# Retention decays: from a mask product per pair to running sums made once and read back as rows

## The reference

```python
q = _l2norm((x @ Wq).reshape(b, seq_len, h, d)).transpose(0, 2, 1, 3)
k = _l2norm((x @ Wk).reshape(b, seq_len, h, d)).transpose(0, 2, 1, 3)
v = (x @ Wv).reshape(b, seq_len, h, d).transpose(0, 2, 1, 3)
dt = jax.nn.softplus(x @ Wa + dt_bias)
alpha = jnp.exp(-jnp.exp(A_log) * dt)
cum_log = jnp.cumsum(jnp.log(alpha + 1e-08), axis=1).transpose(0, 2, 1)
log_l = cum_log[..., :, None] - cum_log[..., None, :]
l_mat = jnp.where(causal, jnp.exp(log_l), 0.0)
scores = jnp.einsum('bhid,bhjd->bhij', q, k) * l_mat
out = jnp.einsum('bhij,bhjd->bhid', scores, v)
...
return out * gate @ Wo
```

## Time and profile before

| | us |
|---|---|
| median of 3 runs (1632.02 to 1636.08) | 1634.42 |
| the profiled execution | 1648.23 |
| its span in the profile | 1646.4 |
| busy in the span: PE 94%, DVE 68%, ACT 54%, POOL 43% | |
| granted TensorE clock, mean over the span | 0.979 |

### The profile page before, as it was taken

The page is one execution under the profiler, slowest core; times in us unless marked ns, Lnnn a source line. Parts: engine busy times, 40 slices in busy tenths (PEclk is TensorE's granted clock), DMA queues, the critical chain, the costliest instruction groups (busy, mean ns, idle before and its releaser), DMA issues. The chain is left out here.

```text
span 1646.4 us, 45308 instructions
## 1 busy us (share of the span) xinstructions
PE 1544.4 (94%) x16414; PEld 1193.2 (72%) x16414; DVE 1121.6 (68%) x1761; ACT 896.3 (54%) x1419; POOL 701.8 (43%) x755
## 2 busy tenths in 40 slices
PE   8998999989999987889999999999999999889998
PEld 4544666679989655457777777777777777668887
DVE  3643545668787468467777777777777777267777
ACT  5463333432222347346666666666666666467776
POOL 0300000577877456443444433444433444166665
PEclk9998999999999999799999999999999999999999
DMA  2028984131110000376655566655556654212211
GB/s 76 1 58 223 249 243 129 39 118 51 64 41 22 1 2 2 90 166 151 145 127 131 129 142 149 147 125 131 129 140 149 149 125 112 52 39 79 69 63 45
DMA packets 53548, 168.84 MB, mean 103 GB/s; under 512 B 12640, under 2 KB 25280, under 8 KB 53472
## 3 DMA queue, kind: packets, MB, share of 16 engines
q1 hardware_dynamic: 51312, 156.30, 38.0%
q10 hardware_dynamic: 2160, 11.52, 2.3%
HBM read 90.27 MB, written 1.03 MB: 55 GB/s over the span
## 5 line engine op out<-in xcount | busy, mean ns | idle before, releaser
L1907 DVE TENSOR_REDUCE hat_tops<-banks 128x1 f32<-128x500 f32 x672 | 442.0, 677 | 151.4 <-PE banks L1653 151.3
L1780 ACT ACTIVATE hat_pb<-banks 125x896 f32<-125x896 f32 x384 | 340.2, 916 | 226.3 <-PE banks L1672 222.2
L1653 PE MATMUL banks<-hat_kh,hat_qm 128*128 128x500 f32 x672 | 298.7, 462 | 3.8 <-DVE hat_tops L1907 3.5
L1672 PEld LDWEIGHTS banks<-hat_q,hat_k 128*125 128x125 f32 x1536 | 219.6, 188 | 74.4 <-issue 31.9
L1672 PE MATMUL banks<-hat_q,hat_k 128*125 128x224 f32 x1536 | 250.5, 286 | 15.8 <-ACT hat_pb L1780 9.2
L1849 POOL CAST hat_kh<-hat_kf 128x500 fp32r<-128x500 f32 x96 | 58.5, 609 | 404.1 <-ACT hat_kf L1793 389.3
L1663 PE MATMUL banks<-hat_pb,hat_vs 125*27 125x168 f32 (+1 forms) x6144 | 166.9, 261 | 0.1
L1663 PEld LDWEIGHTS banks<-hat_pb,hat_vs 125*27 125x27 f32 (+1 forms) x6144 | 132.1, 98 | 44.1 <-issue 24.4
L1226 ACT ACTIVATE ffn_rg<-banks 128x448 f32<-128x448 f32 x128 | 69.9, 546 | 165.6 <-PE banks L1159 165.5
L1653 PEld LDWEIGHTS banks<-hat_kh,hat_qm 128*128 128x128 f32 x672 | 127.7, 191 | 40.9 <-DVE hat_tops L1907 25.5
L2149 DVE TENSOR_TENSOR moe_hl<-moe_hf,moe_hh 128x448 fp32r<-128x448 f32 x128 | 108.5, 887 | 42.3 <-POOL moe_hh L2041 41.6
(11 more groups left out here) (286 smaller groups left out, 3091.3 us busy)
## 6 DMA issues: line engine op xcount, KB each, us to landing
hat_k<-hat_kh SPq DMA_DIRECT2D x256, 187.5 KB, 4.7
hat_ct<-ctxT SPq DMA_DIRECT2D x32, 750.0 KB, 6.2
hat_k<-hat_kl SPq DMA_DIRECT2D x128, 187.5 KB, 4.5
ctx_cx<-ctx SPq DMA_DIRECT2D x32, 672.0 KB
ctx_cd<-ctxT ACTq DMA_DIRECT2D x15, 750.0 KB, 5.7
ffn_cb<-expert_weights SPq DMA_DIRECT2D x8, 896.0 KB, 4.3
moe_cb<-expert_weights SPq DMA_DIRECT2D x8, 896.0 KB, 6.1
moe_raw<-Mw SPq DMA_DIRECT2D x18, 256.0 KB, 3.0
```

Source lines behind the costliest of these rows:

```text
L1653: peak_out.inc(nc.tensor.matmul(g.bank(PK + m % 2)[:, 0:SB], qm[u][:].rearrange("p h i -> p (h i)")[:, r * 128:r * 128 + 128], kh[u][:, c ...
L1672: mm = nc.tensor.matmul(g.bank(2 * (t % 2) + j // 2)[0:SW, (j % 2) * QW:(j % 2 + 1) * QW], k3[u][:, j, t * SW:(t + 1) * SW], q3[u][:, j, : ...
L1780: exped.inc(nc.scalar.activation(pb[t % 6][:].rearrange("p (n i) -> p n i", n=2), g.ps[0:SW, 2 * (t % 2):2 * (t % 2) + 2, 0:2 * QW], ACT.E ...
L1907: peaked.inc(v.tensor_reduce(tops[:, r, n:n + 1], g.bank(PK + m % 2)[:, 0:SB], AX_X, ALU.max))
```

## The change

The running sums of the log decays are made once for all pairs, and each pair's mask product takes them in.

- First block: one product of the selector `until` with all decays (256 columns, fp32) into bank 4, between the first and the second half of the v projections. ACT rounds its negative into `parts`, DVE puts the rounding's remainder beside it, PE turns `parts` in four transposes into bank 5, ACT copies that into `turned` (128 x 4 x 128). SP stores `turned` in DRAM (`sums_dram`), waits for the store, and then issues the four loads of the rows of pairs 0 and 1, all before the block ends.
- POOL fills two tables `hid` (the hiding values for 16 heads; rows 56 to 59 are overwritten by the loads) and `head_of`, and `unit` is no longer the identity: its rows 56 to 59 subtract the loaded rows.
- Second block: SP issues two loads per pair (2 x 16 x 56 numbers each) for pairs 2 to 15, each pair's after PE has finished the masks of the pair two before. PE's first two products read `hid` instead of `hidden` and also wait for the loads; the two fp32 products with `after` and `dm` are replaced by two fp32r products of 32 rows with `turned` and `head_of`. DVE's `dm` is gone, and with it the wait on it.
- The loop `staged` is replaced by `each_pair`, which writes all 18 slots out.

```diff
-    out["after"] = (same & (p[:, None] > p[None])) * 1.0
+    out["until"] = (same & (p[:, None] <= p[None])) * 1.0
+    out["head_in_pair"] = (p[:, None] % H == np.arange(H)[None]) * 1.0
+    rows = np.diag((p % 64 < L) * 1.0)
+    rows[L:L + 2, 0:L] = rows[L + 2:L + 4, 64:64 + L] = -1.0
+    rows[L + 4, L:64] = rows[L + 4, 64 + L:128] = 1.0
+    out["row_of"] = rows
...
+        def load_rows(sp, p):
+            for k in range(2):
+                source = g.sums_dram[p // 4, 32 * (p % 4):32 * (p % 4) + 32, 64 * k:64 * k + L]
+                sp.dma_start(hid[p % 2][L + 2 * k:L + 2 * k + 2].bitcast(F32), source.rearrange("(l h) i -> l h i", l=2)).then_inc(rows_in[p % 2], 16)
...
+                sp.wait_ge(sums_kept, 1)
+                sp.dma_start(g.sums_dram.rearrange("g r c -> r g c"), turned[:].bitcast(F32)).then_inc(sums_stored, 16)
+                sp.wait_ge(sums_stored, 16)
+                sp.wait_ge(cleared, 6)
+                for p in range(2):
+                    load_rows(sp, p)
...
                     if p == 8:
+                        pe.wait_ge(scaled, 3)
+                        pe.wait_ge(s_step, 6)
+                        nc.tensor.matmul(g.bank(4)[:, 0:PAIRS * H], c_["until"], decay[:].rearrange("p a h -> p (a h)"), start=True, stop=True).then_inc(sums_out, 1)
                         pe.wait_ge(limited, CH)
...
+                pe.wait_ge(sums_split, 2)
+                for n in range(4):
+                    mm = nc.tensor.transpose(g.bank(5)[:, n * 128:n * 128 + 128], parts[:, 4 * n:4 * n + 4].rearrange("p a l h -> p (a l h)").bitcast(F32), c_["ident"])
+                mm.then_inc(sums_turned, 1)
...
+                act.wait_ge(sums_out, 1)
+                nc.scalar.activation(parts[:, :, 0, :], g.bank(4)[:, 0:PAIRS * H].rearrange("p (a h) -> p a h", h=H), ACT.Copy, scale=-1.0).then_inc(sums_split, 1)
+                act.wait_ge(sums_turned, 1)
+                nc.scalar.copy(turned[:].rearrange("p g c -> p (g c)"), g.bank(5)).then_inc(sums_kept, 1)
...
+            @block.sync
+            def _(sp):
+                for p in range(2, PAIRS):
+                    d_out.wait(sp, p - 2)
+                    load_rows(sp, p)
...
                         exped.wait(pe, p - 1)
+                        pe.wait_ge(rows_in[u], 32 * (h + 1))
                         for k in range(2):
-                            nc.tensor.matmul(g.ps[:, 4 + k, 0:CW], unit[:], hidden[:], start=True, stop=False)
-                        dmade.wait(pe, p)
+                            nc.tensor.matmul(g.ps[:, 4 + k, 0:CW], unit[:], hid[u][:, 8 * k:8 * k + 8, :], start=True, stop=False)
+                        own_rows = slice(32 * (p % 4), 32 * (p % 4) + 32)
                         for k in range(2):
-                            mm = nc.tensor.matmul(g.ps[:, 4 + k, 0:CW], c_["after"], dm[u][:, 8 * k:8 * k + 8, :], start=False, stop=True)
+                            mm = nc.tensor.matmul(g.ps[:, 4 + k, 0:CW], turned[own_rows, p // 4, :], head_of[own_rows, 8 * k:8 * k + 8, :], start=False, stop=True)
                         d_out.inc(mm)
...
-                    if scores:
-                        d_out.wait(dve, p - 2)
-                        a = decay[:].rearrange("p a h -> p (a h)")[:, bass.ds(p * H, H)]
-                        dmade.inc(nc.vector.tensor_tensor(dm[u][:], spread(a, 2, L), spread(c_["upto"], 1, H), ALU.mult))
...
-                staged(dve, PAIRS, slot)
+                each_pair(dve, slot)
```

More of the change, by code:

```diff
@@ L379, in retention @@
         vm = [sb(f"vm{u}", [128, HG * (D + DH)]) for u in range(2)]
-        unit, hidden = sb("unit", [128, 128], F32R), sb("hidden", [128, CW], F32R)
+        unit, head_of = sb("unit", [128, 128], F32R), sb("head_of", [128, H, L], F32R)
+        hid = [sb(f"hid{u}", [128, H, L], F32R) for u in range(2)]
+        parts, turned = sb("parts", [128, PAIRS, 2, H], F32R), sb("turned", [128, 4, 128], F32R)
+        sums_out, sums_split, sums_turned, sums_kept, sums_stored = (sem(n) for n in ("sums_out", "sums_split", "sums_turned", "sums_kept", "sums_stored"))
+        rows_in = [sem(f"rows_in{u}") for u in range(2)]
+        def load_rows(sp, p):
+            for k in range(2):
+                source = g.sums_dram[p // 4, 32 * (p % 4):32 * (p % 4) + 32, 64 * k:64 * k + L]
+                sp.dma_start(hid[p % 2][L + 2 * k:L + 2 * k + 2].bitcast(F32), source.rearrange("(l h) i -> l h i", l=2)).then_inc(rows_in[p % 2], 16)
         with nc.Block() as block:
@@ L429, in _ @@
                     nc.gpsimd.memset(vm[u][:], 0.0).then_inc(cleared, 1)
-                nc.gpsimd.tensor_copy(unit[:], c_["ident"]).then_inc(cleared, 1)
-                nc.gpsimd.tensor_copy(hidden[:].rearrange("p (h i) -> p h i", i=L), spread(c_["hide_later"], 1, CW // L)).then_inc(cleared, 1)
-                pool.wait_ge(cleared, 4)
+                nc.gpsimd.tensor_copy(unit[:], c_["row_of"]).then_inc(cleared, 1)
+                for u in range(2):
+                    nc.gpsimd.tensor_copy(hid[u][:], spread(c_["hide_later"], 1, H)).then_inc(cleared, 1)
+                nc.gpsimd.tensor_copy(head_of[:], spread(c_["head_in_pair"], 2, L)).then_inc(cleared, 1)
+                pool.wait_ge(cleared, 6)
             @block.scalar
@@ L487, in _ @@
                 dve.wait_ge(scaled, CH)
+                dve.wait_ge(sums_split, 1)
+                nc.vector.scalar_tensor_tensor(out=parts[:, :, 1, :], in0=g.bank(4)[:, 0:PAIRS * H].rearrange("p (a h) -> p a h", h=H), scalar=-1.0,
+                                               in1=parts[:, :, 0, :].bitcast(F32), op0=ALU.mult, op1=ALU.subtract).then_inc(sums_split, 1)
+                dve.wait_ge(sums_split, 2)
         kp = [sb(f"kp{u}", [128, 2 * L]) for u in range(2)]
         qb = [sb(f"qb{u}", [128, 2, HG, L]) for u in range(2)]
-        dm = [sb(f"dm{u}", [128, H, L]) for u in range(2)]
         ee = [sb(f"ee{u}", [128, H, L]) for u in range(2)]
@@ L548, in slot @@
                         scored.inc(mm)
-                staged(pe, PAIRS, slot)
+                each_pair(pe, slot)
             @block.scalar
@@ L1931, in _, with each_pair @@
                 normed.wait(dve, B - 1)
+def each_pair(engine, slot):
+    for p in range(PAIRS + 2):
+        slot(p, p % 2, p // 2, p < PAIRS, 1 <= p <= PAIRS, p >= 2)
 def staged(engine, n, slot):
```

12 lines of the change are left out of this document (6 added, 6 removed).

## The result

The changed kernel takes **1657.97 us** in the median of 4 runs (1653.54 to 1669.1), beside 1634.62 us in 4 runs of the kernel before on the same chip: a ratio of **1.0141, 95% interval 1.0106 to 1.0176**. It is slower by 23.4 us, 17.3 to 28.8, where 7.0 us less were forecast. Its profiled execution takes 1658.55 us, near its median. In the experiments each ratio is taken against the kernel before run beside it (medians 1636.71 to 1640.01 us). One slow execution of experiment 2, 2121.06 us, is left out of its ratio.

A forecast was written before the change was run, and what follows sets the result against it. A ring between PE's masks and ACT's exponential, 3.43 us per pair, was taken as the bound. Pairs -14.7, prologue +6.15 and clock +1.5 summed to -7.0 us: from 1634.4 to 1627.4 us, range 1622 to 1636.

The forecast's parts named there:

- the last rival: Pairs in the second block: TensorE's clock stays at 1.2 GHz, period near 4 us, 1650 us in all; chance 0.02.
- The ring: Per pair, PE's masks to ACT's exponential and back to PE: 3.43 us falls to 2.42 (2.32 to 2.52), gaining 14.7 us.
- the forecast's lower bound: Per pair without a step cost: exponential starts 1.11 us after the masks instead of 2.22, ring 2.32 us.
- The step to 32 rows: In each pair's masks, going from 128-row to 32-row products costs 0.1 us, bounds 0 and 0.2.
- PE's own work: Per pair, PE's masks, line 536 and line 546 together take 2.4 us, level with the ring.
- The clock's price of 1.5 us: Start of the second block: one or two pairs run at 1.2 GHz after PE's idling, costing 1.5 us (0 to 3).
- Prologue: First block: added serial path starts the second block 6.65 us later; 0.5 is recovered, leaving 6.15.
- The store's way: End of the first block: the 256 KB store lands in 1.6 to 3.0 us, taken as 2.2.
- the late loads: Rival in the pairs: row loads land too late, period 3.45 us, no gain, prologue cost stays, 1642.3 us; chance 0.08.
- Writing out the loop: Second block's pair slots: replacing the loop by written-out slots costs nothing.
- A second ring: Rival in the pairs: PE's own work or the scores' ring sets about 2.85 us per pair, 1633.9 us; chance 0.27.
- the forecast case: Whole kernel: main forecast of 1627.4 us, spanning about 1624 to 1631, a fifth above 1629.5; chance 0.55.

The follow-up runs named there:

- experiment 2: Changed kernel with the two 32-row products put on all 128 rows, 96 of them zeros: 1644.32 us, ratio 1.0021 to the kernel before.
- experiment 11: Changed kernel plus one idle fp32 product on all 128 rows at the head of every slot: 1647.45 us, ratio 1.0069 to the kernel before.
- experiment 4: Kernel before with SP held in the first block by three stores, so PE idles ahead of the pairs: 1648.21 us, ratio 1.0043.
- experiments 2 and 3: Changed kernel with those products on 128 rows (1644.32 us); the second also with nine idle PE products before the pairs (1638.64 us, ratio 0.9979).
- experiment 5: Kernel before with its loop of 18 slots written out and nothing else changed: 1637.28 us, ratio 0.9999.

## Why the prediction was wrong

**The step that failed is the last rival**, "The clock stays at 1.2 GHz through the pairs, since PE has less to do: a period near 4, 1650". It came about as described: a period of 4.09, 1658. I gave it 0.02, "PE would be busy for most of every 2.42 us, as it was at the full clock in the stretch of rows 1". The argument takes busy time for what the clock follows, and the runs deny it: PE was busy for 50.00 of 50.00 us at 1.2 GHz (the change, and 64 rows), and for 32.66 of 34.00 at 2.4 GHz (128 rows). What had changed between the earlier trace rows and the new slot is what kind of work made up the busy time: four fp32 passes on all rows gone, two products on 32 rows in their place. The profile before could not have proved the case, but it should have had a chance beside the others: nothing in it showed a stretch of such products at full clock.

**The ring was right, at a clock that it did not get.** With the clock up (experiment 2) the masks' start to the exponential is 1.12 (68.22 to 69.34), where the forecast's lower bound was 1.11, and the slot 2.33, where it was 2.32. The step to 32 rows, put at 0.1 with bounds 0 and 0.2, costs 0.19 (experiment 11): 0.09 ahead of the two products, as the row had shown, and 0.10 between them, where the forecast had named up to 0.11 for weights that aren't loaded beforehand. So the ring of the change is 2.52 at full clock, the upper bound and not the 2.42, and the pairs would have gained 13.2 and not 14.7 (an estimate: 50.96 less 15 x 2.52). The Trainium skill (TensorEngine Tiling (Array Packing), Tiling Modes) says that a change of mode drains TensorE; the 0.09 ahead of the first is the most that this costs here, as the 0.10 stands between two products of one shape.

**At half the clock** I took 3.3 for a ring: 2.20 + 0.92 + 0.29 is 3.4 by the rows above. But the period is 4.09, because PE's own work, level with the ring at 2.4 by my count, becomes longer than it: the masks take 2.09 where 32 rows take 1.20 at full clock, the product with v 1.04 instead of 0.76, the scores 0.96 instead of 0.56, while ACT's 0.92 stays. The first two pitches, 3.16, belong to slots in which PE has no outputs to make yet.

**The clock's price of 1.5 us** (0 to 3) was for a start at 1.2 GHz that ends by itself. In experiment 4 and experiment 2 it does end, after 6.8 and 10.2 us; in the change it lasts through the pairs and some 10 us behind the last exponential. By the rows above the term should have been about 24 (an estimate): 59.45 less 15 x 2.52 in the pairs, 21.6, and 2.5 behind them.

**Prologue.** Forecast 6.15 more up to pair 0's exponential, and part of the clock's 1.5; measured 7.0, in all about right. The store's way was put at 2.2, and SP issued the next transfer 2.3 after it (41.99 to 44.31). The four loads took 2.70 to issue (the row at 44.31) instead of 1.9; the four transposes 0.66 instead of 1.14. PE idled 7.05 where I had 5.8.

**The rivals that stayed away.** PE never waited for row data in the pairs (the waits above; at full clock, experiments 2 and 3), and taking the loads away moved the exponentials by 0.9 us of 39: the late loads are out. Writing out the loop cost nothing at 3.43 (experiment 5), as forecast; at 2.33 the written-out kernels took 38.03 to 39.12 and those with the loop 35.77, 36.50 and 38.13, so the runs don't decide it. The Trainium skill (Runtime: NRT & Kernel Launch, Instruction fetch mechanics) would have the loop pay at a taken branch, and no run here shows that: 50.95 us written out and 50.96 with the loop in the kernel before. A second ring at 2.85 did not appear in any kernel.

**What the forecast would have given with the clock up:** experiment 2 is the change in all but the zero rows and the copies that they need, with a stage of -2.6 us: pairs -12.9, prologue +6.8 (14.05 less 7.27), and +3.6 behind the last exponential, where the clock was at 1.2 GHz again for 6.8 us from 91.8 on. My -7.0 had left out the time behind, and the median of that kernel is no faster than before.

**Three numbers of the forecast were wrong by themselves.** A row load is 7.0 KB and not 3.5, two of them per pair; as 2.5 and 56 KB both land in 1.6, no term moves. The time of the late loads should read 1642.1 (1634.4 and 7.65). And if a fifth of the forecast case lies above 1629.5, it enters the chance of "faster" with 0.8 and not 0.9.

## What to carry to other kernels

A product made cheaper by fewer rows may take from TensorE what keeps its clock up, and at 1.2 GHz that cost here more than it gained (fp32r in place of fp32, on 128 rows, did not take it: experiment 2); a busy share doesn't tell, so read the granted clock beside it in each stretch, and give such an edit a price at half the clock. Zeros up to 128 rows cost no time on PE at the same columns (0.50 us for two products, where 32 rows took 0.60) and the clock came up with them, so try them first. Compare stages of two profiles from the last point that both share: 3.4 us of the profile before were chance, nearly as much as the best kernel gains.

## What the runs showed of the hardware that was not expected

- TensorE stayed at 1.2 GHz for 75.1 us, in the middle 50.00 of which PE was busy for 50.00, with the mix of the change: per slot two fp32r products on 128 rows, two on 32 rows, and the small ones of scores and outputs. With 64 rows it was the same to the tenth of a microsecond; with 128 rows, 96 of them zeros, the clock rose 10.2 us after it had fallen, at the same columns. Where between 64 and 128 rows it turns, and by what the chip judges, was not tried.
- One added fp32 product on 128 rows per slot lifted the clock and shortened the slot from 4.09 to 3.27 us.
- A full clock at the start of the pairs was no protection: it fell in the middle of pair 1 (55.1 us) after PE had been kept busy up to the barrier (and for 2.60 of the 4.10 us between), and for 6.8 us even with 128 rows.
- At 2.4 GHz two products on 32 rows amid products on more rows cost 0.19 us more than two on 128 rows: 0.09 ahead of them, 0.10 between them.
- Unedited code behind the stage took between 1521.8 and 1534.4 us in the profiled executions of this study.
